# Gated linear attention by strips of two heads: state, inner gate, PSUM places, preparation and last row rearranged

## The reference, cut to what matters

```python
xn = layernorm(x)
# s: attention block on xn
h  = rmsnorm(xn) * ln1_w
q, k, v, g = h @ Wq, h @ Wk * 32**-0.5, h @ Wv, h @ Wg + bg      # 16 heads, keys 16 wide, values 32 wide
gk = log_sigmoid(h @ Wkg1 @ Wkg2 + bkg2) / 16                    # Wkg1: 512 x 16, the "inner gate" u = h @ Wkg1
for t:  S = S * exp(gk[t])[:, None] + outer(k[t], v[t]);  o[t] = q[t] @ S        # per head, S is 16 x 32
xm = xn + (silu(g) * normed_per_head(o)) @ Wo
s  = xm + (silu(rms(xm) @ W1) * (rms(xm) @ W3)) @ W2             # hidden width 1408 = 11 blocks of 128
# gate: mixture of 8 low-rank experts on xn
y  = x + s * silu(moe(xn))
```

## Time and profile before

| | us |
|---|---|
| median of 3 runs (1604.48 to 1606.0) | 1604.78 |
| profiled execution | 1603.78 |
| span of its instructions | 1602.0 |
| PE busy | 1577.2 (98%) |
| DVE busy | 851.9 (53%) |
| ACT busy | 567.2 (35%) |
| POOL busy | 164.1 (10%) |

### The profile page before, as it was taken

One profiled execution on the slowest core, in us unless ns is written; L12 is line 12 of the kernel. 1 busy time (PEld: TensorE's weight loads), 2 busy tenths in 40 slices (PEclk: granted clock), 3 DMA queues, 4 the chain that ended last, 5 costly groups with the idle time before them and its releaser, 6 DMA issues.

```text
span 1602.0 us, 30629 instructions
## 1 busy us (share of the span) xinstructions
PE 1577.2 (98%) x12274; PEld 1275.2 (80%) x12274; DVE 851.9 (53%) x1320; ACT 567.2 (35%) x988; POOL 164.1 (10%) x190
## 2 busy tenths in 40 slices
PE   7999999999999999999999999999999999999997
PEld 5788778787777777777777888888888888888886
DVE  5555555467797887978887451331415142241413
ACT  4333334376564655736555411111111111111111
POOL 1632500100220102101020100000000000000000
PEclk9999999999999999999999999999999999999999
DMA  7544333101020211202123423030301203030200
GB/s 159 156 105 105 107 75 88 60 27 41 21 85 0 85 40 45 85 0 85 74 66 123 142 99 132 0 137 0 137 0 44 94 0 137 0 137 0 84 22 27
DMA packets 50700, 113.16 MB, mean 71 GB/s; under 512 B 13321, under 2 KB 24665, under 8 KB 42466
## 3 DMA queue, kind: packets, MB, share of 16 engines
q1 hardware_dynamic: 47906, 99.95, 19.2%
q10 hardware_dynamic: 1152, 8.39, 1.3%
q0 software_dynamic: 1600, 4.25, 1.2%
HBM read 78.98 MB, written 33.59 MB: 70 GB/s over the span
## 4 chain that ended last, share of the span: by engine, by line
PE 90%; DVE 6%; issue 1%; ACT 1%; PEld 1%; DMA 0%; DVEq 0%; SPq 0%; ACTq 0%; PEldq 0%
PE m_ps L1563 9%; PE m_ps L1561 9%; PE m_ps L1562 9%; PE a_ps L161 7%; PE a_ps L163 7%; PE a_ps L162 7%; PE f_ps L161 5%; PE f_ps L163 5%; PE f_ps L162 5%; PE m_ps L1575 4%; PE m_ps L1576 4%; PE m_ps L1577 4%; PE a_att L1310 3%; PE a_ps L1429 2%; PE a_ps L1331 2%
## 5 line engine op out<-in xcount | busy, mean ns | idle before, releaser
L1804 DVE TENSOR_TENSOR m_h<-m_ps,m_silu 128x512 f32<-128x512 f32 x85 | 58.7, 691 | 397.3 <-PE m_ps L1563 397.3
L1561 PE MATMUL m_ps<-m_xshi,m_w 128*128 128x512 f32 x680 | 266.3, 392 | 0.0
L1563 PE MATMUL m_ps<-m_xshi,m_w 128*128 128x512 f32 x680 | 264.7, 389 | 0.0
L1562 PE MATMUL m_ps<-m_xslo,m_w 128*128 128x512 f32 x680 | 264.6, 389 | 0.0
L1868 ACT ACTIVATE m_silu<-m_ps 128x512 f32<-128x512 f32 x85 | 50.8, 598 | 328.9 <-PE m_ps L1563 328.9
L1563 PEld LDWEIGHTS m_ps<-m_xshi,m_w 128*128 128x128 f32 x680 | 127.6, 188 | 26.7
L1561 PEld LDWEIGHTS m_ps<-m_xshi,m_w 128*128 128x128 f32 x680 | 127.7, 188 | 26.3 <-issue 0.2
L1562 PEld LDWEIGHTS m_ps<-m_xslo,m_w 128*128 128x128 f32 x680 | 127.7, 188 | 26.2 <-issue 0.2
L1043 DVE TENSOR_TENSOR a_a<-a_att,causal 128x1024 f32<-128x1024 f32 x64 | 75.2, 1216 | 12.1 <-PE a_att L1310 12.1
L1877 ACT ACTIVATE m_h0hi<-m_h 128x512 fp32r<-128x512 f32 x46 | 29.1, 633 | 136.4 <-DVE m_h L1804 136.4
L1122 POOL TENSOR_TENSOR row<-row,a_r 128x512 f32<-128x512 f32 x32 | 50.9, 1624 | 252.4 <-DMA a_r<-scratch_r 252.4
(11 more groups left out here) (310 smaller groups left out, 3487.1 us busy)
## 6 DMA issues: line engine op xcount, KB each, us to landing
row<-scratch_xn SPq DMA_DIRECT2D x16, 1024.0 KB, 4.9
row<-scratch_xmid SPq DMA_DIRECT2D x16, 1024.0 KB, 7.3
m_xt<-in_L_attn_W SPq DMA_DIRECT2D x33, 256.0 KB, 3.1
f_xt<-in_L_attn_x SPq DMA_DIRECT2D x32, 256.0 KB, 7.6
scratch_xn<-row SPq DMA_DIRECT2D x8, 1024.0 KB, 8.5
scratch_gate<-row ACTq DMA_DIRECT2D x8, 1024.0 KB, 3.9
scratch_xmid<-row SPq DMA_DIRECT2D x8, 1024.0 KB, 3.9
row<-scratch_gate SPq DMA_DIRECT2D x8, 1024.0 KB, 10.6
```

The costliest lines, as they stand in the source:

```text
L1561: pe.matmul(ps, wh, xh, start=k == 0, stop=False)
L1562: pe.matmul(ps, wh, xl, start=False, stop=False)
L1563: ins = pe.matmul(ps, wl, xh, start=False, stop=k == LAST)
L1804: dve.tensor_tensor(h[n], dense.region(f"b{j}"), silu[n], ALU.mult).then_inc(dense.taken_sem(f"b{j}"), 1)
```

## The change

1. `state` becomes 128 x 64 for each group: in each strip of 32 partitions two heads, with two column blocks of 32. VectorE makes it with one product with `parity` (one instruction for both groups) and a decay of 64 columns. Queries times state becomes, for each group, four matmuls of 32 partitions x 64 columns, one for each strip, at partitions 32 x strip and columns 64 x (strip mod 2). Their results stand in two banks, `ps_mix`: strips 0 and 1 (an even quad of heads) in the first, strips 2 and 3 in the second.
2. The transposed keys move into the second bank of `ps_mix`; at c = 1 and 2 they are made behind the next row's part, and ScalarE's copy of them behind its copy of that part; TensorE waits for that copy ahead of the state products.
3. `Regions` takes a table of places: two banks, and the four of `a_att`, which hold `z`, `v1`, `v2`, `g0`, `g1`, `g2` while no chunk uses them. `clear_weights` goes.
4. The inner gate: `wkg1` holds its high part three times and its low part once, so that the product gives all four places; ScalarE copies 64 partitions at once, VectorE makes one difference. In the last row the part `u` of ScalarE is `weights_hi(4, 6)`.
5. TensorE's row loop of `phase_a` is loaded at slot 163 of a fetch block (`head_slot`), with a wait for `g2` of row 0 ahead of it.
6. The preparation's shares: `wk` and `wq` count 2, `wv` 5, shares of 11 from row 2 on, `wkg2` in row 7.
7. Last row of `phase_m`: `down(8)` moves behind `up(10)`; `down(9)` and `down(10)` go block by block; the high and low part of block 10 are kept in `w[0]`; the transposes go to banks 0 to 3.

```diff
-        state = [sb(f"state{n}", [P, GR, HG * VH]) for n in range(2)]
+        state = [sb(f"state{n}", [P, GR, 2 * VH]) for n in range(2)]
...
+        ps_mix = ctx.enter_context(nc.psum_tensor("a_mix", [P, 2, 512], F32))[:]
...
+        places = {result: n for n, results in enumerate((
+            ["k0", "ds0", "var0", "q0", "ds2", "var2", "var3", "v3", "o0", "o2"],
+            ["k1", "u", "ds1", "var1", "q1", "ms", "v0", "g3", "o1", "o3"],
+            ["z0", "g0"], ["z1", "g1"], ["v1", "g2"], ["v2"])) for result in results}
...
-                        for g in range(GR):
-                            ins = dve.tensor_tensor(new[:, g, :].rearrange("p (h o v) -> p h o v", o=2, v=VH),
-                                                    bcast(ds[:, g], 1, HG // 2),
-                                                    bcast(hmask.rearrange("p (h o) -> p h o", o=2), 3, VH), ALU.mult)
+                        dve.tensor_tensor(new.rearrange("p g (o v) -> p g o v", v=VH), ds,
+                                          bcast(bcast(parity, 1, GR), 3, VH), ALU.mult).then_inc(dense.taken_sem(f"ds{c}"), 1)
...
-                        for quad in range(QD):
-                            g, first_head = quad * HQ // HG, quad * HQ % HG
-                            pe.matmul(ps[:, quad, :], state[c % 2][:, g, first_head * VH:(first_head + HQ) * VH],
-                                      qhat[:, gcs[g], :], start=quad == 0, stop=True, skip_group_check=True)
+                        for g in range(GR):
+                            for strip in range(4):
+                                rows, at = slice(H32 * strip, H32 * (strip + 1)), H64 * (strip % 2)
+                                pe.matmul(ps[2 * g + strip // 2][at:at + H64], state[c % 2][rows, g, :],
+                                          qhat[rows, gcs[g], :], start=g == 0, stop=True, skip_group_check=True,
+                                          tile_position=(H32 * strip, at))
...
+                    for part in (("k0", "k1"), ("u",), ("q0",), ("q1",))[c]:
+                        ahead(part)
+                    if 0 < c < NC - 1:
+                        pe.wait_ge(*mix.taken(c - 1, i))
+                        turned_keys(i, c)
...
+                    if 0 < c < NC - 1:
+                        pe.wait_ge(*turned.taken(c, i))
...
-                dve.tensor_copy(u[0:RANK], ps).then_inc(count.sem("uhi"), 1)
-                dve.tensor_copy(u[64:64 + RANK], ps).then_inc(count.sem("uhi"), 1)
-                dve.tensor_copy(u[96:96 + RANK], at.region("u")[32:32 + RANK]).then_inc(count.sem("uhi"), 1)
+                low = slice(2 * RANK, 3 * RANK)
                 dve.wait_ge(*count.at("uhi", i))
+                dve.tensor_tensor(u[low], at.region("u")[low], u[low].bitcast(F32), ALU.subtract).then_inc(at.taken_sem("u"), 1)
...
+                act.activation(u[0:4 * RANK], at.region("u")[0:4 * RANK], ACT.Copy).then_inc(count.sem("uhi"), 1)
...
-    cost = {"wkg1": 0, "wk": 1, "wq": 1, "wv": 4, "wg": 2, "wo": 2}
+    cost = {"wkg1": 0, "wk": 2, "wq": 2, "wv": 5, "wg": 2, "wo": 2}
...
-        w["statistics"](pool, 1 + max(done[n] - 1, 0) // 8)
+        w["statistics"](pool, 1 if name == "wkg1" else 2 + (done[n] - 1) // 11)
...
+            pe.wait_ge(*dense.taken(f"g{LAST - 1}", 0))
+            loop_parts(pe, NB, parts, body, skip=front.tensor(pe), first=False, slot=163)
...
+                if isinstance(i, int) and i == NB - 1:
+                    for j in rest:
+                        up(i, j)
+                        if j < FT - 2:
+                            down(pe, i, j - 1)
+                    down(pe, i, FT - 3)
+                    for m in range(KT):
+                        for j in (FT - 2, FT - 1):
+                            down(pe, i, j, (m,))
+                    ahead("up0")
+                    turn_last(i)
+                    return
```

More of the change, by code:

```diff
@@ L58, with __init__ @@
 class Regions:
-    def __init__(self, counts, name, regions, order, early=()):
+    def __init__(self, counts, name, regions, order, early=(), places=None):
         self.counts, self.name, self.regions = counts, name, regions
@@ L65, in __init__ @@
         for n, result in enumerate(order):
-            r = n % len(regions)
+            r = places[result] if places else n % len(regions)
             used[r] += 1
@@ L169, in loop, with loop_parts @@
     loop_parts(eng, n, {None: first}, lambda i, ahead: body(i, lambda: ahead(None)), peel)
-def loop_parts(eng, n, parts, body, peel=False, before=None, skip=None, first=True):
+def loop_parts(eng, n, parts, body, peel=False, before=None, skip=None, first=True, slot=None):
     for part, work in parts.items() if first else ():
@@ L182, in loop_parts @@
         body(0, lambda part: parts[part](1))
-    with eng.bass.Fori(1 if peel else 0, n - 1, engines=bass.OrderedEngineSet([eng.engine]), hint_back_edge=True) as i:
+    with eng.bass.Fori(1 if peel else 0, n - 1, engines=bass.OrderedEngineSet([eng.engine]), hint_back_edge=True,
+                       head_slot=None if slot is None else {eng.engine: slot}) as i:
         body(i, lambda part: parts[part](i + 1))
@@ L850, in phase_a @@
         assert GR == 2 and NC == 4
[L852 to L855 removed]
+        order = [("k0", ["k0"]), ("k1", ["k1"]), (None, ["ds0"]), ("u", ["u"]), (None, ["var0", "ds1"]),
+                 ("q0", ["q0"]), (None, ["var1", "ds2"]), ("q1", ["q1"]), (None, ["var2", "ms"]),
+                 ("z", zs), ("v0", values[:1]), (None, ["var3"]), ("v1", values[1:]), ("g", gates),
                  (None, outs), ("body", [])]
+        places = {result: n for n, results in enumerate((
+            ["k0", "ds0", "var0", "q0", "ds2", "var2", "var3", "v3", "o0", "o2"],
+            ["k1", "u", "ds1", "var1", "q1", "ms", "v0", "g3", "o1", "o3"],
+            ["z0", "g0"], ["z1", "g1"], ["v1", "g2"], ["v2"])) for result in results}
         early = {part: results for part, results in order if part}
[L858 to L859 removed]
+        dense = Regions(count, "dense", psum + [ps[:, strip].rearrange("p g o t -> p (g o t)") for ps in ps_att for strip in range(2)],
+                        sum((results for _, results in order), []), sum(early.values(), []), places)
+        turned = Regions(count, "kt", [ps_mix[:, ODD, GR * P:]], list(range(NC - 1)))
         att = Regions(count, "att", ps_att, [f"{c}_{n}" for c in range(NC) for n in range(2)])
[L861 removed]
+        mix = Regions(count, "mix", [ps_mix[:, :, 0:QD // 2 * P]], list(range(NC)))
         LAST = KT - 1
         mean8 = sb("mean8", [P, 8], F32R)
[L865 removed]
         parity, s_parity = sb("parity", [P, 2]), outer.enter_context(nc.semaphore("a_parity"))
@@ L1409, in body @@
                     pe.wait_ge(*mix.free(c, i))
-                    ps = mix.region(c).rearrange("p (q t) -> p q t", t=P)
+                    ps = [mix.region(c)[:, (EVEN, ODD)[quad % 2], quad // 2 * P:(quad // 2 + 1) * P] for quad in range(QD)]
+                    if 0 < c < NC - 1:
+                        pe.wait_ge(*turned.taken(c, i))
                     if c > 0:
@@ L1463, in tensor @@
             f.tensor(pe, first_row)
[L1464 to L1465 removed]
+            pe.wait_ge(s_parity, 4)
+            parts["v0"](0)
+            for m in range(KT):
+                pe.wait_ge(*f.dense.taken(f"u{m}", NB - 1))
+            for part in ("v1", "g"):
                 parts[part](0)
[L1467 removed]
+            pe.wait_ge(*dense.taken(f"g{LAST - 1}", 0))
+            loop_parts(pe, NB, parts, body, skip=front.tensor(pe), first=False, slot=163)
         stage.count, stage.dense, stage.att, stage.mix, stage.early = count, dense, att, mix, early
@@ L1564, in up_products, with hidden_parts, down @@
             return ins
-        def down(pe, i, j):
+        def hidden_parts(i, j):
+            if isinstance(i, int) and i == NB - 1 and j == FT - 1:
+                return [flat(w[0][:, 0, part]) for part in range(2)]
+            return h_hl[j % 2]
+        def down(pe, i, j, ms=range(KT)):
             pe.wait_ge(*count.at("hlo", i, j + 1))
             pe.wait_ge(s_wlo, 3 * j + 3)
-            rh, rl = h_hl[j % 2]
-            for m in range(KT):
+            rh, rl = hidden_parts(i, j)
+            for m in ms:
                 if j == 0:
@@ L1593, in gpsimd @@
             def gpsimd(pool):
-                zs, (v0,), (_, v2, v3), (g0, g1, g2, g3) = (a.early[part] for part in ("z", "v0", "v1", "g"))
-                pass_over(pool, a.dense, zs + [v0, v2, v3, g1, g2, g0, g3], NB)
+                pass_over(pool, a.dense, ["v3", f"g{LAST}"], NB)
             @staticmethod
@@ L1833, in body @@
                     dve.wait_ge(*acc.ready(f"t{t}", i))
-                    dve.tensor_tensor(xt[:, t, :], acc.region(f"t{t}"), xt[:, t, :],
+                    last = isinstance(i, int) and i == NB - 1
+                    dve.tensor_tensor(xt[:, t, :], last_turned[t] if last else acc.region(f"t{t}"), xt[:, t, :],
```

(4 more changed lines are left out.)

156 lines of the change are left out of this document (72 added, 84 removed).

## The result

The changed kernel takes 1608.27 us (median of 21 runs, 1603.17 to 1614.47) against 1605.52 of the kernel before (21 runs, 1603.17 to 1607.05): a ratio of 1.0018, 95% interval 1.0009 to 1.0026. Forecast were 1590.8, faster, with a range up to 1599.5. So instead of 14 us less it is 3 us more, and 17 us have to be found. The profiled execution is one of the slower ones, 1613.62 with a span of 1611.6; its first 30 us hold 1.9 us more of waits at the start (L687 and L147) than that of before.

What follows compares the result with a forecast made beforehand. TensorE, busy 98% of the span, was taken as the bound. Terms -6.1 - 3.0 - 2.0 + 0 - 2.9 = -14.0 from the profiled 1603.8 gave 1589.8, plus 1.0 for the median 1590.8; range 1587.0 to 1599.5.

Steps and rivals of the forecast that it cites:

- Part 1, state by strips: State products of `phase_a`: four rounds, 0.63 in place of 0.98 us for each c > 0; with the keys' copy -6.1.
- the first rival: State products: strips that share a PSUM bank go in turn, 10.6 us more, 1601.4; chance 0.12.
- The keys' copy: At c = 1 and 2 state products wait 0.07 for ScalarE, plus 0.04 shape change; last row gives back about 0.5.
- The third rival: ScalarE's copy of the keys is late: 0.3 at 16 places, 4.8 us, about 1595.6; chance 0.09.
- Part 2, places: PSUM places in `phase_a`: waits for banks go, 1.5 us in row 0 and 0.25 a row over six rows; -3.0.
- Preparation: `phase_f`: the 1.7 wait for VectorE's normalisation and 0.3 at the inner gate go, new overlap taken 0; -2.0.
- The end: End of the kernel: blocks finish in turn, sum with `x` starts near 1593.9 in place of 1596.82; -2.9.
- Part 5, the slot: PE's row loop at slot 163: may save one `issue` wait or cause one on entry, -1.2 to +1.2, taken 0.
- The second: PE's row loop at its new slot stalls once a pass: 7 x 1.22 = 8.5 us, 1599.3; chance 0.10.
- the fourth: PE's row loop stalls two or three times each pass: 17.1 to 25.6 us, 1607.9 to 1616.4, slower; chance 0.06.

Runs made afterwards that it cites:

- slot 40: The changed kernel with TensorE's row loop of `phase_a` beginning at slot 40 of a fetch block instead of 163: 1596.94 us, ratio 0.9946.

## Why the prediction was wrong, point by point

- **Part 1, state by strips: right.** 0.63 a chunk forecast, 0.59 measured with 0.10 more ahead of them; four rounds, and the first rival (shared banks in turn, 0.12) is out: it would have been over 1.0. With the moved transposes 0.29 less at c = 1, forecast 0.24.
- **The keys' copy: right.** No wait in rows 0 to 6; in the last row 0.4 at L1442, which the profile calls `issue`, forecast 0.5 (there a longer part is ahead of the copy on ScalarE). The third rival is out.
- **Part 2, places: right.** The waits of the earlier trace rows are gone and so is the slow start of the earlier trace rows. That start lies in row 1 and comes back in rows 1 to 6; I had named them row 2 and rows 2 to 7, with the same count of six. A row without `issue` waits is 64.6 instead of 65.7: 1.1 to 1.2 less, forecast 0.83 + 0.25 = 1.08.
- **Preparation: right in size, one bound used.** `phase_f` ends 2.3 earlier at slot 40, forecast 2.0. The new overlap that I took at 0 (bounds 0 to 1.7) costs 0.8.
- **The end: right.** The sum with `x` starts 2.8 earlier, counted from the last product; forecast 2.9.
- **Part 5, the slot: this is the step that failed.** "The slot may save that one wait or cause one on entry: bounds -1.2 to +1.2, taken 0." It caused eleven waits in rows 1 to 6, 11.7 us, each with 0.2 more behind it, 13.9 together, and a fall of the clock that took 1.8; by the medians slot 40 gives back 11.3. The other five of the 16 waits, in rows 0 and 7, are not the slot's. I had the length of the loop (some 1970), the slot and the rule on 2048, and by them a loop of nine blocks; I let the loop of before, "no pass through the loop shows such a wait", speak against it. That trace could not: it does not tell whether the loop was loaded anew or not until one looks at the fetch queue, where 28 packets say that it was not. The Trainium skill, page "Runtime: NRT & Kernel Launch", section "Instruction fetch mechanics", speaks of a window of two pages for a taken branch, where the prediction has the whole 2048 instructions. The trace is with the prediction: at slot 40 the loop branches back over eight blocks without a wait.
- **The rivals.** The second (one stall in each pass, 8.5 us, 0.10) and the fourth (two or three, 14 to 21, 0.06) name the mechanism. The fourth is nearest in size: 14 to 21 waits of 1.22 in seven passes forecast, 13 of 1.10 in rows 0 to 6 measured, and its 1607.9 to 1616.4 holds the 1608.3. Its "against", that 65 us for 1970 instructions leave a fetch much time, is a mean over stretches that differ by a factor of 18: 256 instructions pass in 1.62 us at L1310 and in 29 at the wide products. That the total agrees is in part luck: 6 of the 17 us missing have the reason in the next point.
- **Rows 0 and 7.** Even where the loop stays loaded 6 us are missing. 4 to 5 of them are first-time fetches that I had not seen as something that the change could move; at slot 40, 1.6 are two waits for VectorE in row 7, chunk 3 (L1042, L1047) that no step of mine had, and one fall of the clock (3.4 us from 838.1) took about 1.7 more. Without such terms 1596.8 would be close to 1591.

## What to carry to other kernels

When an edit lengthens an unrolled loop, count its instructions, two for each product and four in fp32, and those that wait or set registers (60 here), add the slot at which it begins, and compare with what the engine holds: here 2040 stayed loaded and 2064 did not. Then look at the fetch queue's packets on the page, which tell in one number whether a loop is loaded again in each pass. And price a fetch not by the mean pace of the loop but by its fastest 256 instructions; the same nine fetches cost nothing in one kernel and 2 us a row in another. Look at the granted clock behind each such wait as well, and check a wait called `issue` against the engines that the next instruction may wait for.

## What the hardware showed beyond what was expected

- Being loaded again can be free: the kernel before at slot 163 brings 9 blocks in each row and runs at 0.9991 (0.9981 to 1.0) of its time.
- The same instructions took 1596.7 to 1620.9 us by the slot of one loop alone, 1.5%, with the waits shown only as `issue`.
- A wait of 1.4 us or more of PE within `phase_a` was in 14 of 37 cases followed by 3.4 us at 1.2 GHz, and one such fall made row 6 of the changed kernel 1.8 us longer.
- Strips of 32 rows that write one bank of PSUM in pairs run four at once: sixteen products in 0.59 us. The Trainium skill, page "TensorEngine Tiling (Array Packing)", section "Restrictions and Gotchas", says that row tiles cannot access one bank at the same time; for strips that write different partitions of the bank, as here, the trace shows no cost.
- An `addr_align` without a loop behind it costs a wait of 1.5 to 1.9 us at the jump in all four runs.
- The fastest kernels found are the changed one with the loop at slot 0, 24, 40 or 56, 1596.7 to 1596.9 us, ratio 0.994.
